# Value and sum products in column halves behind every score, in a two-layer gated cross-attention kernel

## The reference

```
def xattn_1(qkv, y):                      # qkv = layernorm(x), y = ctx (4 x 1601 x 512)
    q = qkv.reshape(bs * 16, 32, 512)     # 64 heads of 32 channels
    k = v = y.reshape(bs * 16, 32, 1601)  # keys and values are the same numbers
    weight = softmax(einsum('bct,bcs->bts', q * scale, k * scale))
    return einsum('bts,bcs->bct', weight, v)
x = x + tanh(g_xattn[1]) * xattn_1(layernorm(x), ctx)
```

## Time and profile before

| | us |
|---|---|
| median of 3 runs | 1844.12 (1843.73 to 1844.43) |
| profiled execution, device time | 1841.3 |
| its span, first to last instruction | 1839.5 |
| mean granted TensorE clock in the span | 0.959 |
| the second cross-attention's 16 groups, 741.0 to 1564.2 in the span | 823.2 |

### The profile page before, as it was taken

One profiled execution on the slowest core, in us unless ns is written; L12 is line 12 of the kernel. 1 busy time (PEld: TensorE's weight loads), 2 busy tenths in 40 slices (PEclk: granted clock), 3 DMA queues, 4 the chain that ended last, 5 costly groups with the idle time before them and its releaser, 6 DMA issues. The chain is left out here.

```text
span 1839.5 us, 22129 instructions
## 1 busy us (share of the span) xinstructions
PE 1658.9 (90%) x7540; PEld 800.2 (44%) x7568; DVE 1147.0 (62%) x1529; ACT 760.9 (41%) x1241; POOL 843.0 (46%) x340
## 2 busy tenths in 40 slices
PE   5999999898777876899999999899999997799898
PEld 2454444444433333444444444444444432344443
DVE  3669989884455557676766676667676630444543
ACT  1321211211543431566666666566666665111110
POOL 0022234544221125577778888677777877000000
PEclk9999999899899995999999999999999999799999
DMA  8232223322111115444333334444433310400000
GB/s 320 80 120 77 83 93 96 103 100 79 39 30 35 34 41 137 113 114 112 77 96 89 98 97 113 114 113 113 113 88 90 77 46 1 95 23 0 23 23 23
DMA packets 134316, 152.57 MB, mean 83 GB/s; under 512 B 59694, under 2 KB 101826, under 8 KB 134214
## 3 DMA queue, kind: packets, MB, share of 16 engines
q1 hardware_dynamic: 129222, 140.76, 29.3%
q10 hardware_dynamic: 4992, 10.49, 1.7%
HBM read 73.42 MB, written 10.76 MB: 46 GB/s over the span
## 5 line engine op out<-in xcount | busy, mean ns | idle before, releaser
L1352 DVE TENSOR_REDUCE c_piece_max<-c_unit 128x1 f32<-128x804 f32 x512 | 485.0, 984 | 241.0 <-PE c_unit L1490 238.4
L1448 ACT ACTIVATE c_prob<-c_scores 128x512 f32<-128x512 f32 (+1 forms) x832 | 473.3, 596 | 267.3 <-PE c_scores L1507 250.5
L1287 POOL TENSOR_TENSOR c_prob_sum<-c_prob_sum,c_prob 128x2048 f32<-128x2048 f32 x96 | 439.4, 4577 | 12.0 <-ACT c_prob L1448 6.0
L1507 PE MATMUL c_scores<-c_queries,c_keys 98*128 98x512 f32 (+1 forms) x832 | 354.8, 443 | 32.7 <-ACT c_prob L1448 17.4
L1490 PE MATMUL c_unit<-c_khigh,c_qdiag 128*128 128x402 f32 x1024 | 303.2, 381 | 20.1 <-DMA c_qdiag<-c_qhigh 10.1
L1490 PEld LDWEIGHTS c_unit<-c_khigh,c_qdiag 128*128 128x128 f32 x1024 | 186.6, 198 | 150.1 <-DVE c_piece_max L1352 90.1
L1507 PEld LDWEIGHTS c_scores<-c_queries,c_keys 98*128 98x128 f32 (+1 forms) x832 | 152.4, 186 | 202.0 <-ACT c_prob L1448 141.3
L1516 PE MATMUL c_out<-c_prob,c_VT 128*32 128x512 f32 (+1 forms) x1664 | 220.8, 610 | 0.0
L641 PE MATMUL a_S<-a_ctxT,a_xnT 128*128 128x401 f32 x512 | 190.7, 517 | 7.2 <-ACT a_prob L598 3.9
L671 PE MATMUL a_o<-a_ctx,a_probT 128*128 128x512 f32 (+1 forms) x416 | 181.2, 592 | 0.0
L1287 POOL TENSOR_TENSOR c_prob_sum<-c_prob 128x2048 f32<-128x2048 f32 x16 | 73.5, 4592 | 121.1 <-ACT c_prob L1448 121.1
(11 more groups left out here) (196 smaller groups left out, 1975.0 us busy)
## 6 DMA issues: line engine op xcount, KB each, us to landing
c_keys<-c_khigh SPq DMA_DIRECT2D x128, 200.2 KB, 3.0
c_k<-in_keys SPq DMA_DIRECT2D x16, 801.0 KB, 6.3
c_keys<-c_k SPq DMA_DIRECT2D x64, 200.2 KB, 3.0
a_ctx<-in_ctx SPq DMA_DIRECT2D x12, 1024.0 KB, 6.8
c_VT<-in_values SPq DMA_DIRECT2D x16, 768.0 KB
a_ctxT<-in_ctxT SPq DMA_DIRECT2D x12, 802.0 KB, 4.7
c_queries<-c_qhigh SPq DMA_DIRECT2D x128, 64.0 KB, 2.6
a_weights<-in_L_ffn_weight SPq DMA_DIRECT2D x3, 1408.0 KB, 14.7
```

What stands on the lines that cost most here:

```text
L1287: nc.gpsimd.tensor_tensor(psum4[:], a[:], prob[(j * MC + c) % RING][:], ALU.add).then_inc(sums_taken, 2 if i == 1 else 1)
L1352: nc.vector.tensor_reduce(piece_max[j % 2][:, k // 2, k % 2:k % 2 + 1], U[bank(unit)][:, :, 0:PIECE], axis=AX.XY, op=ALU.max).then_inc(uni ...
L1448: nc.scalar.activation(prob[(j * MC + c) % RING][0:w, h, :], STp[h % 2][0:w, :], ACT.Exp, scale=SCALE).then_inc(exp_done, 1)
L1507: nc.tensor.matmul(STp[h % 2][0:w, :], K[p][:, h, c * P:c * P + w].bitcast(F32R), Q[p][:, h, :].bitcast(F32R), start=True, stop=True).then ...
```

## The change

Value and sum products are issued for 256 of the 512 columns at a time (`columns`, `half` 0 or 1; the first value block and the first sum block of a group stay whole). A plan (`placed`) gives each piece a place behind one of the group's 52 scores, numbered 4 to 55 as 4c + h, at most one piece behind a score. The three closing blocks change order: the last value block goes behind scores 1 and 2 of the next group's chunk 0 (places 53 and 54), and the last sum block and the block of GpSimd's sum, in halves, behind the first four scores of the next group's pass (places 4 to 7). The units are now dealt out against a running sum of weights (0.53 for a half, 0.36 for a unit). A new signal `out_done` tells ScalarE that `O` is complete; ScalarE copies it before the exponentials of chunk 1 and no longer amid those of chunk 0. VectorE's reciprocals stand before units 3 to 6 and no longer before 0, 2, 4 and 6.

```diff
--- before.py
+++ after.py
@@ -1124,6 +1124,7 @@
         scores_ready = sem("c_scores_ready")
         exp_done = sem("c_exp_done")
         pv_done = sem("c_pv_done")
+        out_done = sem("c_out_done")
         den_done = sem("c_den_done")
         sums_taken = sem("c_sums_taken")
         rden_ready = sem("c_rden_ready")
@@ -1380,8 +1381,8 @@
                     for i in range(PARTS):
                         finish(g - 1, i)
                 for u, unit in enumerate(stream):
-                    if before and u % 2 == 0 and u // 2 < PARTS:
-                        finish(g - 1, u // 2)
+                    if before and 3 <= u < 3 + PARTS:
+                        finish(g - 1, u - 3)
                     if later and unit[2:] == (j + 2, 0):
                         moments_begun(g + 3)
                         dve.wait_ge(stat_steps, 2 * (g + 3) + 1)
@@ -1429,14 +1430,14 @@
                 nc.scalar.copy(nparts[:].bitcast(F32R)[:, :, :, 0].rearrange("p t h -> p h t"), nmax[:]).then_inc(nhigh_ready, 1)
 
             def take_out(g):
-                act.wait_ge(pv_done, PV0 + (g + 1) * CHUNKS)
+                act.wait_ge(out_done, g + 1)
                 wait(act, x_added, g)
                 nc.scalar.activation(taken[:], O[:], ACT.Copy, scale=gates[:, 1:2]).then_inc(out_taken, 1)
 
             def exponentials(g, j, c):
                 w = P if c < MC - 1 else ML
                 for h in range(H):
-                    if c == 0 and h == 2 and (not isinstance(g, int) or g > 0):
+                    if c == 1 and h == 0 and (not isinstance(g, int) or g > 0):
                         take_out(g - 1)
                     act.wait_ge(scores_ready, SCORES0 + g * EXPS + H * c + h + 1)
                     if h == 0:
@@ -1506,37 +1507,74 @@
                 pe.wait_ge(exp_done, g * EXPS + H * c + h + 1)
                 nc.tensor.matmul(STp[h % 2][0:w, :], K[p][:, h, c * P:c * P + w].bitcast(F32R), Q[p][:, h, :].bitcast(F32R), start=True, stop=True).then_inc(scores_ready, 1)
 
-            def out(g, j, c):
-                w = P if c < MC - 1 else ML
+            WHOLE = 2
+
+            def columns(half):
+                return slice(0, D) if half == WHOLE else slice(half * D // 2, (half + 1) * D // 2)
+
+            def out(g, j, c, half):
+                w, cols = P if c < MC - 1 else ML, columns(half)
                 if c == 0:
                     pe.wait_ge(v_loaded[j % 2], 2 * turn(g, j % 2))
                     wait(pe, out_taken, g)
-                pe.wait_ge(exp_done, EXPS0 + g * EXPS + H * (c + 1))
+                if half != 1:
+                    pe.wait_ge(exp_done, EXPS0 + g * EXPS + H * (c + 1))
                 for h in range(H):
-                    last = nc.tensor.matmul(O[h * CH:(h + 1) * CH, :], VT[j % 2][0:w, c, h * CH:(h + 1) * CH],
-                                            prob[(j * MC + c) % RING][0:w, h, :], start=c == 0, stop=c == MC - 1)
-                return last
-
-            def den(g, j, c):
-                k = ML if c == MC - 1 else P
+                    last = nc.tensor.matmul(O[h * CH:(h + 1) * CH, cols], VT[j % 2][0:w, c, h * CH:(h + 1) * CH],
+                                            prob[(j * MC + c) % RING][0:w, h, cols], start=c == 0, stop=c == MC - 1 and half == 1)
+                if half > 0:
+                    if c == MC - 1:
+                        last.then_inc(out_done, 1)
+                    elif c not in SUMMED:
+                        last.then_inc(pv_done, 1)
+
+            def den(g, j, c, half):
+                w, cols = P if c < MC - 1 else ML, columns(half)
                 if c == SUMMED[0]:
                     wait(pe, rden_ready, PARTS * g)
                 for h in range(H):
-                    last = nc.tensor.matmul(DEN[h * CH:(h + 1) * CH, :], ones32[0:k, :], prob[(j * MC + c) % RING][0:k, h, :],
+                    last = nc.tensor.matmul(DEN[h * CH:(h + 1) * CH, cols], ones32[0:w, :], prob[(j * MC + c) % RING][0:w, h, cols],
                                             start=c == SUMMED[0], stop=False)
-                return last
-
-            def den_of_sum(g):
-                pe.wait_ge(sums_taken, (g + 1) * NP)
+                if half > 0:
+                    last.then_inc(pv_done, 1)
+
+            def den_of_sum(g, half):
+                cols = columns(half)
+                if half == 0:
+                    pe.wait_ge(sums_taken, (g + 1) * NP)
                 for h in range(H):
-                    last = nc.tensor.matmul(DEN[h * CH:(h + 1) * CH, :], ones32[:], psum4[:, h, :], start=False, stop=True)
-                last.then_inc(den_done, 1)
-
-            def out_and_den(g, j, c):
-                last = out(g, j, c)
-                if c in SUMMED:
-                    last = den(g, j, c)
-                last.then_inc(pv_done, 1)
+                    last = nc.tensor.matmul(DEN[h * CH:(h + 1) * CH, cols], ones32[:], psum4[:, h, cols], start=False, stop=half == 1)
+                if half == 1:
+                    last.then_inc(den_done, 1)
+
+            def last_sums(g, j, i):
+                if i < 2:
+                    den(g, j, MC - 1, i)
+                else:
+                    den_of_sum(g, i - 2)
+
+            def placed(before):
+
+                gaps = {}
+                for c in range(1, MC):
+                    for b in {1: [], 2: [0], 3: [1, 2]}.get(c, [c - 1]):
+                        at = 4 * c + (1 if b == c - 1 else 0)
+                        if b == 0:
+                            gaps.setdefault(at + 1, []).append(("out", b, WHOLE))
+                            continue
+                        gaps.setdefault(at, []).append(("out", b, 0))
+                        gaps.setdefault(at + (2 if b not in SUMMED else 1), []).append(("out", b, 1))
+                        if b == SUMMED[0]:
+                            gaps.setdefault(at + 2, []).append(("den", b, WHOLE))
+                        elif b in SUMMED:
+                            gaps.setdefault(at + 2, []).append(("den", b, 0))
+                            gaps.setdefault(at + 3, []).append(("den", b, 1))
+                for half in range(2):
+                    gaps.setdefault(4 * MC + 1 + half, []).append(("out", MC - 1, half))
+                if before:
+                    for i in range(4):
+                        gaps.setdefault(4 + i, []).append(("last", None, i))
+                return gaps
 
             def slot(g, j, main, nxt, more, later):
                 stream = unit_stream(g, j, main, nxt, more)
@@ -1547,43 +1585,43 @@
                     for h in range(H):
                         score(0, 0, 0, h)
                     return
-                first_gap, gaps = 0, H * MC
-                per_gap = max(len(stream), UNITS) / (gaps - first_gap)
-                gap = given = 0
-
-                def units():
-                    nonlocal gap, given
-                    gap += 1
-                    upto = round((gap - first_gap) * per_gap)
-                    while given < min(len(stream), upto):
+                before = not isinstance(g, int) or g > 0
+                gaps = placed(before)
+                HALF, PAIR = 0.53, 0.36
+                weights = {gap: sum(HALF * (1 + (what != "last" and half == WHOLE)) for what, b, half in parts) for gap, parts in gaps.items()}
+                per_gap = (sum(weights.values()) + PAIR * max(len(stream), UNITS)) / (H * MC)
+                given, done = 0, 0.0
+
+                def products(gap):
+                    nonlocal given, done
+                    for what, b, half in gaps.get(gap, []):
+                        if what == "out":
+                            out(g, j, b, half)
+                        elif what == "den":
+                            den(g, j, b, half)
+                        else:
+                            last_sums(g - 1, (j - 1) % TURN, half)
+                        done += HALF * (1 + (what != "last" and half == WHOLE))
+                    upto = (gap - 3) * per_gap
+                    while given < len(stream) and (done + PAIR / 2 <= upto or gap == 4 * MC + 3):
                         unit = stream[given]
-                        if unit[0] == "rows" and upto <= AHEAD + ROWS_AT:
+                        if unit[0] == "rows" and gap < ROWS_GAP:
                             break
                         rows(unit) if unit[0] == "rows" else pair(unit)
                         given += 1
-
-                outs = {1: [], 2: [0], 3: [1, 2]}
-                for c in range(1, MC):
+                        done += PAIR
+
+                ROWS_GAP = 4 + round((AHEAD + ROWS_AT) * H * MC / UNITS)
+                for c in range(1, MC + 1):
                     for h in range(H):
-                        score(g, j, c, h)
-                        if h == 1:
-                            for b in outs.get(c, [c - 1]):
-                                out_and_den(g, j, b)
-                        units()
-                if nxt:
```

(21 more changed lines are left out.)

## The result

The changed kernel takes 1899.59 us (median of 4 runs, 1897.63 to 1900.26) against 1843.92 for the kernel before beside it (1842.88 to 1844.43): a ratio of 1.0301, with a 95% interval from 1.0283 to 1.0319. It is slower by 55.7 us; the prediction said 43. The profiled execution took 1897.63 us, with a span of 1895.9.

The account below looks back on a forecast made before the run. TensorE, busy 90% of the span, was taken as the bound. A group: 41.0 work + 11.5 excursions + 1.4 stalls = 53.9 against 50.35; +47 us over groups 1 to 13, +42.5 with the ends, gave 1887 us, range 1836 to 1920.

Parts of the forecast that it names:

- Halves take half: TensorE's value and sum products: a 256-column piece takes 0.43 us, half a block's 0.86, so halving adds 0.
- The price is 0.32 and belongs to the switch: TensorE: each excursion into 32-column blocks costs 0.32 us whatever its length; 36 instead of 12 add 7.7 us a group.
- rival A: TensorE's switch costs in proportion to the piece, 0.16 for a half: faster, 1801 us; chance 0.12.
- The estimate of 0.21: Price of a TensorE excursion from the skill's drain and weight-load figures: group 50.0 us, kernel some 1829 us.
- The stalls' remainder, "1.4 us in all": TensorE's waits left in a steady group: 1.4 us instead of 5.5, so stalls give back 4.1 us.
- The part for scores, 0.8: Second cross-attention: two scores wait some 0.4 us each where ScalarE does something else, such as the key cast.
- The part for doubled pairs, 0.6: VectorE: reciprocals before four neighbouring units, and two pairs in one place eight times, make pairs wait 0.6 us a group.
- Moved steps are covered: Later closing sums, reciprocals, gain and output copy cost nothing; GpSimd's gain may come 2 to 3 us later.
- The ends: Groups outside the long stretch: group 0 +2 us, group 14 -0.5, group 15 -6.
- B: Stalls stay at 5.5 us through VectorE's reciprocals and doubled pairs or GpSimd's gain: group 58.0, 1948 us; chance 0.09.
- C: Another engine holds the group at 50.3 us, switches fall into TensorE's waits: 1838 us; chance 0.06.

Follow-up runs that it names:

- experiment 2: Changed kernel with each block issued as its two halves directly behind one another, in 19 places: 1893.0 us, ratio 1.0259 to the kernel before.
- Experiment 10: Against experiment 4, halves in 19 places issued as two quarters of 128 columns with a pair between them: 1963.0 us, ratio 1.0656 to the kernel before.
- experiment 5: Changed kernel with each reciprocal over 4 of 128 columns, the others holding a constant: 1896.2 us, ratio 1.0295 to the kernel before.
- experiment 4: Changed kernel, halves kept, with units dealt out by count so that no place gets two pairs: 1871.4 us, ratio 1.0149 to the kernel before.
- experiment 7: Changed kernel with GpSimd's gain moved behind one more pair of its adds: 1901.3 us, ratio 1.0324 to the kernel before.
- experiment 3: Changed kernel with the old runs of whole blocks and old dealing of units; closing sums, output copy and reciprocals stay moved: 1840.0 us, ratio 0.9981 to the kernel before.
- experiment 9: Changed kernel with whole blocks in 15 excursions, places of pieces and units picked one by one: 1823.1 us, ratio 0.9908 to the kernel before.
- experiment 11: Experiment 9 with one unit a place later, group 14 placed as in experiment 6, group 15 as in the change: 1816.4 us, ratio 0.9881 to the kernel before.
- experiment 6: Changed kernel with whole blocks in 19 places and units dealt by count: 1841.3 us, ratio 1.0000 to the kernel before.

## Why the prediction was right, and which term was off

The forecast was slower, by the price of more excursions; 1899.6 lies in its range.

- **Halves take half: right.** A half piece takes 0.57 until the next start, as forecast; experiment 2 shows 1.00 against 0.99 for two halves and a whole.
- **The price is 0.32 and belongs to the switch: right.** 36 excursions instead of 12 are +7.7 us a group. Experiment 10 measures 0.328 with pieces of 128 columns. This ended rival A, which needed a price under 0.22. The estimate of 0.21, worked out from the Trainium skill's page TensorE: Matmul & The Clock Gate (Part 2, step 4, and LDWEIGHTS), would have made the group 50.0, and the measured 0.32 decides. That changing the tiling mode drains TensorE, as the Trainium skill's page TensorEngine Tiling (Array Packing) says under Key Properties, agrees with the trace: the load of the score behind a run starts with its matmul, after 0.84 us in which no load ran.
- **The stalls' remainder, "1.4 us in all": the term that was off.** It is 2.5, so the steady group is 55.04 and not 53.9. Groups 1 to 13 grew by 58.0 and not by 47, which is 11.0 of the 13.9 us by which the span missed the forecast; the ends below are the other 2.9. The part for scores, 0.8, was too large: one score waits by more than the reading, 0.33. The part for doubled pairs, 0.6, was too small: 0.37, 0.60 and 0.65 at the places shown and three of about 0.1 behind waiting pairs make some 1.9. And the reason was wrong: not the reciprocals (experiment 5: no change in the group) but pairs dealt two to a place, at the places shown behind VectorE's statistics and its row copy. That the dealing is the cause is shown by experiment 4, which takes it away and leaves 0.7; what the statistics and the copy add was not tested.
- **Moved steps are covered: right in time, not in each wait.** The gain waits 4.7 us, in the 3 to 5 forecast. ScalarE does wait 1.6 us for GpSimd's add, which the prediction called covered, but experiment 7 removes both waits and gains nothing, and experiment 3 shows the moved steps at no cost.
- **The ends.** Group 0 +3.3 (forecast +2), group 14 +0.4 (-0.5), group 15 -7.9 (-6). Left out was the end of the stage: +2.6 behind the last copy of `O`, because the closing sums now follow the last value block and four reciprocals of 3.4 us together stand alone there; experiment 5, which shortens them, has 280.8 us there, as before (281.0). Of group 15's 7.9 us some 2.0 are the clock, for which the forecast had no term: it was granted at 0.93 there before and at 1.00 after. The rows below are of the kernel before, from the table by stretches and from TensorE's timeline. Behind scores that had waited for exponentials the granted clock fell to the lower of its two levels, 1.2 GHz. One block took 1.63 us there (1515.24 to 1516.87), and a run of two took 3.22, where 0.99 and 1.85 are the readings at 1.00. Without these 2.0 some 5.9 are left, about the 6 of the forecast.

```profile
1515.50:1522.40 6.90, 6.64 (x28) 1.67 (x20) 0.00 (x0) 2.62 (x5) 6.82 (x4) 0.51 0.01 2
```

```profile
1519.56 3.29 PE L1516 MATMUL c_out<-c_prob,c_VT 128*32 128x512 f32 x16
1522.78 0.73 PE L1507 MATMUL c_scores<-c_queries,c_keys 98*128 98x512 f32 x2
```

- **Rivals B and C: no.** Stalls fell from 5.5 to 2.5, so B's 58.0 did not come; and the group moved by 4.7 us, so no other engine held it, against C.

So the gain that the change aims at exists, up to 5.5 - 0.7 = 4.8 us a group with even dealing. It is bought with 24 excursions, 7.7 us. Worked out from these, it would break even at 0.20 us an excursion. Experiments 9 and 11 take the cheaper side: nearly as few excursions as before, and half the stalls.

## What to carry to other kernels

Where one engine issues two kinds of work that use its array in different shapes, count the changes of shape and read the price of one from start to start before cutting pieces smaller: here 0.32 us each, which is three quarters of a half piece's 0.43. Cutting finer to feed a second engine did not pay here by itself: with units dealt by count, whole blocks in 19 places have a group of 51.05 and halves in 36 places one of 53.17, and even in group 15, which has no pairs, halves took only 0.5 us less than whole blocks one behind a score. Choose places for whole pieces first. Deal out filler work by the time of the engine that consumes it, since two pairs in one place cost more here than the reciprocals that the prediction suspected.

## What the runs showed of the hardware

- The price of going from matmuls of 128 columns of the array to 32-column strips and back does not depend on the length of the piece: 0.31 to 0.32 us, from start to start, around pieces of 256, 512 and 1024 columns (after, experiment 2, before), and 0.33 by the groups of experiments 4 and 10 for pieces of 128, if their matmuls take a quarter of a block's 0.86.
- Matmuls of 32 output partitions cost by their columns: eight rows of 512 take 0.86 us, and two pieces of 256 back to back take 1.00 until the next start, a whole block 0.99. A piece of 256 takes 0.57 and one of 128 takes 0.36 until the next start; less the 0.14 of leaving, that is 0.43 and 0.22.
- The wait of a weight load in the list is not yet a wait of the array: in experiment 6 pairs' loads wait 10.9 us for VectorE in a group that has 4.0 us of stalls in all.
- Open: what would take away the remaining 2.8 us of stalls in experiments 9 and 11. The diagonal's transfer was argued and fell. From start to start, in the group of experiment 9 three second scores come 0.34 late each, as in experiment 6, and two pairs 0.28 and 0.33 (954.13 to 954.65 and 971.72 to 972.39); the rest lies in small pieces at many places.
